# VectorE takes over the subtraction of the maxima for the fourth score bank

## The reference

```python
q = xn @ Wq + bq; k = ctx @ Wk + bk; v = ctx @ Wv + bv
scores = einsum('bqhd,bkhd->bhqk', q, k) / sqrt(8)       # 64 x 64 per head and sequence, masked in layer 1
probs = softmax(scores, axis=-1)                         # exp(s - max) / sum
out = einsum('bhqk,bkhd->bqhd', probs, v)
x = x + out @ Wo + bo                                    # then a layer norm in layer 1
```

## Time and profile before

| | us |
|---|---|
| median of 3 runs | 525.36 |
| lowest, highest | 525.24, 525.47 |
| the profiled execution's own time | 528.26 |
| span that its trace covers | 526.5 |

### The profile page before, as it was taken

One profiled execution on the slowest core, in us unless ns is written; L12 is line 12 of the kernel. 1 busy time (PEld: TensorE's weight loads), 2 busy tenths in 40 slices (PEclk: granted clock), 3 DMA queues, 4 the chain that ended last, 5 costly groups with the idle time before them and its releaser, 6 DMA issues.

```text
span 526.5 us, 17248 instructions
## 1 busy us (share of the span) xinstructions
PE 466.7 (89%) x7014; PEld 379.8 (72%) x7014; DVE 345.1 (66%) x865; ACT 307.3 (58%) x738; POOL 291.8 (55%) x359
## 2 busy tenths in 40 slices
PE   2899999999999999878728697999999999999875
PEld 1577777777778777767726576888888888878664
DVE  6778765677778777335427284968777776767642
ACT  1378777677678777627522446465665555554531
POOL 5465875778878777676553263545443545441220
PEclk9999999999999999989858698999999999999998
DMA  9950000000000000000000000000000000000000
GB/s 297 219 193 3 4 2 2 2 3 2 3 3 2 4 3 1 1 1 2 1 0 1 1 3 2 1 13 2 12 2 3 11 2 13 1 14 1 12 2 20
DMA packets 12278, 11.43 MB, mean 22 GB/s; under 512 B 5160, under 2 KB 10152, under 8 KB 12200
## 3 DMA queue, kind: packets, MB, share of 16 engines
q1 hardware_dynamic: 11624, 9.01, 6.5%
q10 hardware_dynamic: 576, 1.32, 0.7%
HBM read 9.29 MB, written 1.05 MB: 20 GB/s over the span
## 4 chain that ended last, share of the span: by engine, by line
PE 65%; POOL 11%; issue 11%; DVE 7%; ACT 5%; DMA 1%; POOLq 0%; DVEq 0%; ACTq 0%
PE ps L462 7%; PE ps L635 6%; PE ps L745 5%; PE ps L476 4%; PE ps L651 4%; PE ps L444 4%; PE ps L673 4%; PE ps L452 4%; PE ps L643 3%; PE ps L630 3%; PE ps L730 2%; POOL rstd L1544 2%; PE ps L768 2%; PE ps L402 2%; PE ps L681 2%
## 5 line engine op out<-in xcount | busy, mean ns | idle before, releaser
L1220 DVE TENSOR_REDUCE negm<-ps 128x8 bf16<-128x512 f32 x96 | 59.6, 683 | 26.4 <-PE ps L444 26.4
L845 ACT ACTIVATE shared<-ps 128x512 f32<-128x512 f32 x96 | 57.1, 601 | 21.1 <-PE ps L462 19.4
L1617 POOL TENSOR_TENSOR wide<-wide,cv 128x1024 f32<-128x1024 f32 x24 | 45.4, 1893 | 30.6 <-DVE wide L1199 30.6
L462 PE MATMUL ps<-cst,p 128*128 128x128 f32 x384 | 58.8, 276 | 0.4 <-ACT shared L845 0.4
L1544 POOL TENSOR_TENSOR rstd<-veps,neghalf 128x2 f32<-128x2 f32 x40 | 29.0, 724 | 53.5 <-DVE veps L1244 33.9
L839 ACT ACTIVATE p<-ps 128x512 f32<-128x512 f32 x96 | 54.5, 596 | 4.2 <-PE ps L452 4.2
L462 PEld LDWEIGHTS ps<-cst,p 128*128 128x128 f32 x384 | 45.2, 141 | 16.1 <-issue 9.5
L1665 POOL TENSOR_TENSOR probs<-p,rc 128x512 f32<-128x512 f32 x32 | 33.0, 1043 | 39.5 <-DVE rc L1430 39.5
L1030 ACT ACTIVATE late<-ps 128x512 f32<-128x512 f32 x32 | 17.3, 593 | 40.3 <-PE ps L768 40.0
L651 PEld LDWEIGHTS ps<-wo,late 128*128 128x128 f32 x256 | 32.2, 199 | 3.6 <-issue 2.8
L651 PE MATMUL ps<-wo,late 128*128 128x128 f32 x256 | 32.7, 283 | 2.2 <-ACT late L1030 2.2
(11 more groups left out here) (192 smaller groups left out, 1219.9 us busy)
## 6 DMA issues: line engine op xcount, KB each, us to landing
late<-in_mask_l SPq DMA_DIRECT2D x2, 512.0 KB, 11.0
result<-x_all SPq DMA_DIRECT2D x8, 128.0 KB, 1.8
x_all<-in_x_tok SPq DMA_DIRECT2D x1, 768.0 KB, 7.0
wide<-in_ctx_t SPq DMA_DIRECT2D x1, 768.0 KB, 8.9
rv<-in_rv ACTq DMA_DIRECT2D x1, 768.0 KB, 8.0
wa<-in_wa SPq DMA_DIRECT2D x1, 512.0 KB, 10.2
w<-in_w SPq DMA_DIRECT2D x2, 256.0 KB, 6.4
wq<-in_wq SPq DMA_DIRECT2D x1, 512.0 KB, 7.7
```

What stands on the lines that cost most here:

```text
L462: ins = nc.tensor.transpose(bank[:, c * 128:c * 128 + 128], p3[:, n % 3, c * 128:c * 128 + 128], ident)
L845: A_(pt[:, w % 2, r, :], ring_of("p", w, r), ACT.Copy).then_inc(sm["act_pt"], 1)
L1220: V.tensor_reduce(negm[:, n % 4, :], ps[:, S_BANK[r], :].rearrange("p (a k) -> p a k", k=S), AX.X, ALU.max, negate=True).then_inc(sm["dve_ ...
L1617: P.tensor_tensor(r_op[:, w % 2, :, :], k_t[:, w % 2, :].unsqueeze(1).to_broadcast([128, 4, GT]), head_masks.unsqueeze(2).to_broadcast([12 ...
```

## The change

In every turn, PE's fourth `subtract_max` is dropped. In its place DVE gets a new function, `subtract_last(w)`, behind its four `smax` and ahead of `evac_v`: a tensor_tensor addition of bank 3 in PSUM and the broadcast `negm`, written to `probs` in SBUF (two slots of 128 x 512 fp32, unused in these passes before). The fourth exponential waits for the new semaphore `dve_sub` and reads `probs`, not the bank. The counts of `pe_sm` go by three per turn instead of four. Nothing else moves.

```diff
@@ -577,7 +577,6 @@
                     weigh_values(w - 1)
                 subtract_max(w, 1)
                 subtract_max(w, 2)
-                subtract_max(w, 3)
                 transpose_probs(w, 0)
@@ -833,10 +832,14 @@
             def exps(w, r):
                 n = RG * w + r
-                act.wait_ge(sm["pe_sm"], n + 1)
+                if r < RG - 1:
+                    act.wait_ge(sm["pe_sm"], (RG - 1) * w + r + 1)
+                else:
+                    act.wait_ge(sm["dve_sub"], w + 1)
                 if n >= 3:
                     act.wait_ge(sm["pe_pt"], n - 2)
-                A_(p3[:, n % 3, :], ps[:, S_BANK[r], :], ACT.Exp, scale=SC8).then_inc(sm["act_exp"], 1)
+                A_(p3[:, n % 3, :], ps[:, S_BANK[r], :] if r < RG - 1 else probs[:, w % 2, :], ACT.Exp, scale=SC8)\
+                    .then_inc(sm["act_exp"], 1)
@@ -1215,10 +1218,20 @@
             def smax(w, r):
                 n = RG * w + r
                 dve.wait_ge(sm["pe_s"], w + 1)
-                if n >= 4:
-                    dve.wait_ge(sm["pe_sm"], n - 3)
+                if w >= 1 and r < RG - 1:
+                    dve.wait_ge(sm["pe_sm"], (RG - 1) * (w - 1) + r + 1)
+                if w >= 1 and r == RG - 1:
+                    dve.wait_ge(sm["dve_sub"], w)
                 V.tensor_reduce(negm[:, n % 4, :], ps[:, S_BANK[r], :].rearrange("p (a k) -> p a k", k=S), AX.X,
                                 ALU.max, negate=True).then_inc(sm["dve_max"], 1)
+
+            def subtract_last(w):
+                dve.wait_ge(sm["dve_max"], RG * w + RG)
+                if w >= 2:
+                    dve.wait_ge(sm["act_exp"], RG * (w - 1))
+                V.tensor_tensor(probs[:, w % 2, :].rearrange("p (a k) -> p a k", k=S),
+                                ps[:, S_BANK[RG - 1], :].rearrange("p (a k) -> p a k", k=S),
+                                negm[:, RG - 1, :].unsqueeze(2).to_broadcast([128, NP, S]), ALU.add).then_inc(sm["dve_sub"], 1)
@@ -1278,6 +1291,7 @@
                 if now:
                     for i in range(RG):
                         smax(w, i)
+                    subtract_last(w)
                 if w == 0:
                     evac_v(0)
                 if w + 1 < NW:
```

More of the change, by code:

```diff
@@ L228, in build @@
             ln0_mv ln0_ve ln0_r ln0 m_bias m3_split
-            pe_in act_in pe_qk act_q dve_k pool_k pe_v dve_v pe_s dve_max pe_sm act_exp pe_pt act_pt pe_pv act_ot
+            pe_in act_in pe_qk act_q dve_k pool_k pe_v dve_v pe_s dve_max dve_sub pe_sm act_exp pe_pt act_pt pe_pv act_ot
             pe_ot dve_rc dve_atok pe_at act_at pe_o pool_res dve_y dve_st dve_mv dve_ve pool_r pool_yn pool_yg pool_x
```

## The result

| | before | after |
|---|---|---|
| median, us | 525.41 | 539.45 |
| lowest, highest of 4 runs each | 525.24, 527.76 | 538.66, 540.61 |
| the profiled execution's own time | 528.26 | 539.15 |
| span that its trace covers | 526.5 | 537.3 |

The ratio over all the runs is 1.0258, with a 95% interval from 1.0224 to 1.0293 (the ratio of the two medians alone is 1.0267). By the medians the change costs 14.0 us. The forecast was slower, by 10.8 us to 536.2, with a range up to 539.0: the direction came out, the size was 3.2 us short, and the median lies 0.45 above the range. So the result lies at the very edge of what I had allowed for.

What follows compares the result with a forecast made beforehand. PE looked full (49.00 of 49 us), but a PE-DVE loop through L385 sets the turn: 2.0 early + 9.0 (15 x 0.60) - 0.1 = 10.9 more, 539.2 profiled, 536.3 as median; stated 536.2, range 532.5 to 539.

Steps and rivals of the forecast that it cites:

- The room of 0.27 us: Gap from DVE's last evac_v copy to PE's L385; shrinks to a 0.15 wait, so L385 comes 0.60 later per turn.
- The 0.68 us: Predicted length of DVE's new 128 x 512 addition, taken from a reduction reading 512 from PSUM; bounds 0.60 and 0.85.
- The saved product: PE's dropped subtraction, 0.22 per turn, 5.3 us at most; claimed lost in L385's wait for the copies.
- The sum of the early turns: L385's delay over turns 0 to 6: 2.3 us after turn 3, back at about 2.0 by turn 6.
- rival 5: PE's 0.8 us stand each turn lowers its clock, stretching PE's work 0.5 per turn, 10 us in all: 546; chance 0.04.
- The offset from the profiled execution to the median: Whole kernel: the median lies 2.9 us below the profiled 528.26, so 539.2 becomes 536.3.
- PE's time alone (520.1): Only PE's work counts: each turn 0.22 shorter, 5.3 us faster, 520.1; chance 0.04.
- The rule of the Trainium skill: Optimize the engine with highest occupancy first: PE, 49.00 of 49 us, so moving work to DVE gains 5.3 us.
- The wash: Copies delayed by only near 0.12, so L385 comes on time and the time stays unchanged; chance 0.03.
- The cheap addition: DVE's new instruction costs as little as another reduction: 0.48 per turn, 534.1; part of the range, no separate chance.
- the dear one: DVE's new instruction delays copies by 0.97, so 0.85 per turn, 540.9; chance beyond 539: 0.06.
- the exponential out of SBUF: ACT's fourth exponential, reading SBUF, some 0.1 longer; 2 us on top if its 0.7 of cover were gone.

Runs made afterwards that it cites:

- extra512: Kernel before, keeping all four products on PE, plus an unused 128 x 512 addition on DVE behind the maxima, ahead of evac_v: 539.36 us, ratio 1.0265.
- neither: Changed kernel without the addition: bank 4's maxima subtracted neither on PE nor on DVE, the exponential reads the bank as it is; 524.46 us, ratio 0.9974 to kernel before.
- turn0: Changed kernel, but in turn 0 alone the addition stands behind the copies of evac_v(0): 537.04 us, ratio 1.0192 to the kernel before.
- after2: The changed kernel run once more, nothing altered: 537.90 us, ratio 1.0208 to the kernel before.
- mixed: Turns 0 to 6 as in the kernel before; from turn 7 DVE does three maxima, copies, fourth maxima, addition: 523.05 us, ratio 0.9937 to it.
- between: Changed kernel with evac_v ahead of the fourth maxima and the addition on DVE, in all turns: 524.02 us, ratio 0.9971 to the kernel before.
- behind: Changed kernel with the same addition moved behind the evac_v copies on DVE: 525.10 us, ratio 0.9979 to the kernel before.
- two: Changed kernel with the third bank's subtraction also on DVE and the copies behind two maxima: 531.02 us, ratio 1.0083 to the kernel before.

## Why the prediction was right, and where it was short

**The room of 0.27 us** decided, as said. L385 waits, DVE's copies are named 21 times (I had said 22; in turn 6 L385 starts 0.14 behind them, but no idle time is shown) with 14.9 us in total (I had said some 15), it starts 0.15 behind the last copy, and nothing behind it changes (4.29 for 4.27). The copies come 0.73 later, not 0.72, and a turn is 8.75 long, not 8.72. Over turns 7 to 21 that is 9.5, not 9.0.

**The 0.68 us** for the addition was 0.691. The 0.04 for its wait and the overlap of 0.08 came out.

**The saved product** is lost in the wait: shown by extra512, which costs as much without the saving, and by neither, where the saving stands alone and yields 0.09 per turn.

**The sum of the early turns is the step that failed.** "That is 2.3 so far" and "by turn 6 the delay is back at about 2.0" measured 3.4 at both turns 3 and 6 (3.9 and 3.8 counted from the first maxima). I had looked for a falling clock (rival 5) in every turn, where PE stands some 0.8 us; there it stayed at 1.00. It fell at the one place that I did not price: turn 0, where my own step made L385 wait 0.72 longer on top of a wait that was there already. The term that failed is thus the low clock in turn 0, put at nothing and worth 1.6 us; turn0, which keeps the clock at 1.00, has 2.2 at turn 6 against my 2.0. Counted from the first maxima the sum is 10.9 + 1.6 (clock) + 0.2 (the other early turns) + 0.5 (fifteen times 0.64, not 0.60) + 0.1 (the last two turns) = 13.3, which is what the passes have.

**The offset from the profiled execution to the median** was the second miss. I took 528.26 - 525.36 = 2.9 as something that stays. The runs of the kernel before spread from 524.6 to 528.5, and both of its traces happen to be of executions at 528.3. Behind the passes the granted clock varies from one execution to the next. From 212 to 320 us before, and from 225 to 333 us after:

```profile
212.00:320.00 108.00, 77.97 (x815) 66.39 (x803) 54.76 (x156) 49.52 (x138) 59.86 (x80) 0.84 0.00 1
```

```profile
225.00:333.00 108.00, 78.37 (x803) 66.62 (x803) 55.48 (x156) 50.07 (x139) 59.52 (x80) 0.86 0.00 1
```

From the last maxima to the end of the span it is 320.7 us before and 318.6 after, and between 317.0 and 321.4 in all the traces. So the two profiled executions differ by 10.9 us, just as I had summed up, but that is luck: 12.9 in the passes met 2.1 less behind them. The medians differ by 14.0. That leaves 1.1 over the passes' 12.9, which is within what the part behind them varies by; I have nothing that shows another cause. after2, the changed kernel once more, has a clock of 0.84 from 225 to 333 us, where the first trace has 0.86. The spread of the total goes with the mean granted clock of the whole execution: of the 22 runs of the kernel before beside mixed, the fastest five (524.6 to 524.8) have 0.973, the slowest two (528.2) 0.961 and 0.964. What sets the clock behind the passes was not tried.

**The rivals.** PE's time alone (520.1) is refuted for this case: 5.3 us of work were taken from the engine that was busy 49.00 of 49 us, and the passes got 12.9 us longer. The rule of the Trainium skill that I had put beside it ("Perfetto Trace Analysis", section "Identifying the Most-Contended Engine") I had read too simply. For TensorE the same section doesn't go by the busy share of the matmuls: its headroom is to be judged by the FLOPs done against the peak and by the busy share of the weight loads. In 99 to 148 us PE's weight loads were busy for 37.33 us, DVE for 36.12 and POOL for 38.96, so by this measure PE didn't stand out, and the rule gives no case for the step. With the same work placed elsewhere, PE's 0.22 per turn comes almost whole (0.21 in between, 0.20 in mixed). The wash did not happen. The cheap addition (0.48 per turn) and the dear one (0.85) miss 0.64 on either side. For the exponential out of SBUF I had feared 0.1; it lasts 631 ns in place of 593, and no wait came of it.

## What to carry to other kernels

Before moving work to an engine with idle time, look at the place in its order where the work lands, and measure the room there: from the end of what comes behind it to the start of whoever waits for that. What exceeds the room goes one for one into a loop like this one, while work saved on the waiting engine ahead of the wait is worth nothing. The same addition cost 14 us ahead of the copies and nearly nothing behind them (0.09 per turn gained in behind as in neither, which has no addition, with the passes 1.0 us apart), and together with the fourth maxima behind the copies, from turn 7 on, it made the kernel 0.6% faster. Look at the first turns by themselves, too: 1.6 of the 13.3 us came from one long wait in turn 0 and the low clock behind it.

## What the hardware showed that I had not expected

- One stand of PE of 1.69 us, in turn 0, was followed by a granted clock of 0.50 in 25 to 27 us and 0.70 in 27 to 29, and the work up to the next scores took 1.2 us longer. Four traces have such a fall in their first turn: after and after2 (stands of 1.69 and 1.68), extra512 (1.16) and two (1.50, at another line). In the other nine, where the longest stand of turn 0 is 0.96 or less, the clock there is 1.00. The length of the stand alone doesn't decide it: later stands of 1.54 (between, 60.8 us) and 1.34 (behind, in the same turn) left the clock at 1.00. What turn 0 has beside its long stand was not tried.
- A matmul that really waits for DVE starts 0.14 to 0.16 behind the end of the last copy, which the timeline need not show as idle time of PE, since the rows ahead of it overlap the gap.
- The median of one and the same kernel moved by 1.5 us from one set of four runs to another, while its passes repeated within 0.1 us.
